# The quaternion memory read: POOL adds the components of two groups in pairs, PE sums two parts instead of four

## The reference, cut to what matters

```python
keys = (x @ Wk.T + bk).reshape(B, L, 32, 4)
keys = keys / jnp.maximum(norm(keys), 1e-12)
values = (x @ Wv.T + bv).reshape(B, L, 32, 4)
bound = quat_mul(values, keys)
memory = jnp.cumsum(bound, axis=1)
retrieved = quat_mul(memory, quat_conj(keys)).reshape(B, L, D)
retrieved = retrieved / jnp.sqrt(positions)[None, :, None]
normed = layernorm(retrieved) * ln_g + ln_b
return x + (normed @ Wo.T + bo)
```

## Time and profile before

| | us |
|---|---|
| time, median of 3 runs | 853.07 |
| lowest and highest of them | 850.7, 856.16 |
| the profiled execution: its time | 854.02 |
| the profiled execution: its span | 852.2 |
| PE busy in the span | 751.8 |
| DVE busy | 611.0 |
| POOL busy | 495.9 |
| ACT busy | 471.5 |

### The profile page before, as it was taken

How to read it: one execution, slowest core, us unless ns; L and a number is a source line. 1 busy time by engine, 2 the same in 40 slices (tenths; PEclk the granted TensorE clock), 3 DMA queues, 4 the chain that set the end, 5 groups by cost and what they waited for, 6 DMA issues and landing times.

```text
span 852.2 us, 14331 instructions
## 1 busy us (share of the span) xinstructions
PE 751.8 (88%) x3937; PEld 566.2 (66%) x3938; DVE 611.0 (72%) x1398; ACT 471.5 (55%) x951; POOL 495.9 (58%) x518
## 2 busy tenths in 40 slices
PE   4999999989674699917899987999999999999997
PEld 2444555545454699916888876787878787878785
DVE  3799999999843255534788775869686878787774
ACT  3465664556321477713666654666657565656453
POOL 3686776778545144423777764556565565655564
PEclk9999999999655799966999998999999999999999
DMA  8600000000001144520000006363829191918280
GB/s 234 226 2 1 0 1 2 12 4 10 13 26 35 44 123 117 144 62 25 13 14 1 1 2 142 60 145 70 166 48 190 28 197 31 191 44 174 49 165 13
DMA packets 40563, 60.19 MB, mean 71 GB/s; under 512 B 4033, under 2 KB 20033, under 8 KB 40241
## 3 DMA queue, kind: packets, MB, share of 16 engines
q1 hardware_dynamic: 38224, 54.73, 28.1%
q0 software_dynamic: 2272, 4.67, 1.6%
HBM read 51.11 MB, written 8.28 MB: 70 GB/s over the span
## 4 chain that ended last, share of the span: by engine, by line
PE 35%; DVE 9%; issue 3%; ACT 2%; DMA 1%; POOL 1%; POOLq 0%; DVEq 0%; SPq 0%; ACTq 0%
PE c_m L1498 3%; PE c_m L1500 3%; PE c_m L1499 3%; PE c_m L1463 2%; PE c_r L1479 2%; DVE c_bound L1797 2%; PE c_v L1498 1%; PE c_v L1499 1%; PE c_v L1500 1%; PE c_k L1498 1%; PE c_r L1549 1%; PE c_r L1552 1%; PE c_r L1550 1%; PE c_k L1500 1%; PE c_k L1499 1%
## 5 line engine op out<-in xcount | busy, mean ns | idle before, releaser
L2025 POOL TENSOR_TENSOR d_hid_lo<-c_bound,d_hid_hi 128x512 fp32r<-128x512 f32 x136 | 175.4, 1291 | 143.5 <-ACT d_hid_hi L1936 141.6
L1936 ACT ACTIVATE d_hid_hi<-c_bound 128x512 fp32r<-128x512 f32 x136 | 85.0, 625 | 38.8 <-DVE c_bound L1797 37.5
L867 POOL TENSOR_TENSOR a_rs<-a_r,a_state 128x512 f32<-128x512 f32 x64 | 75.1, 1183 | 37.5 <-DVE a_state L564 22.5
L564 DVE TENSOR_TENSOR_SCAN a_state<-a_decay,a_state,a_vb 128x512 f32<-128x512 f32 x64 | 80.9, 1266 | 0.1
L1071 POOL DMA_INDIRECT results<-b_y_row,b_result_row x39 | 37.2, 953 | 54.1 <-DVE b_y_row L1025 54.1
L1788 DVE TENSOR_TENSOR c_m<-c_bound,c_m 128x512 f32<-128x512 f32 x64 | 44.3, 692 | 24.0 <-PE c_m L1500 18.1
L1788 DVE TENSOR_TENSOR c_v<-c_bound,c_v 128x512 f32<-128x512 f32 x64 | 44.3, 692 | 21.9 <-PE c_v L1500 16.3
L1498 PE MATMUL c_m<-d_x_hi,d_hi 128*128 128x512 f32 x136 | 56.3, 414 | 3.7 <-DVE c_bound L1797 3.7
L1016 DVE TENSOR_TENSOR b_hidden<-b_h,b_b 128x512 f32<-128x512 f32 x39 | 27.0, 691 | 40.7 <-PE b_h L979 40.7
L1926 ACT ACTIVATE c_bound<-c_m 128x512 f32<-128x512 f32 x60 | 35.7, 595 | 33.6 <-PE c_m L1500 33.0
L1926 ACT ACTIVATE c_bound<-c_k 128x512 f32<-128x512 f32 x60 | 35.7, 595 | 33.3 <-PE c_k L1500 32.8
(11 more groups left out here) (310 smaller groups left out, 2159.4 us busy)
## 6 DMA issues: line engine op xcount, KB each, us to landing
d_w_wide<-pair_weights SPq DMA_DIRECT2D x64, 512.0 KB, 12.4
b_w<-in_w SPq DMA_DIRECT2D x2, 2048.0 KB, 11.7
d_w_wide<-in_moe SPq DMA_DIRECT2D x32, 102.0 KB
b_xin<-rows_in SPq DMA_DIRECT2D x39, 64.5 KB, 1.8
d_w_wide<-results SPq DMA_DIRECT2D x8, 256.0 KB, 2.8
out<-c_read SPq DMA_DIRECT2D x8, 256.0 KB, 2.2
a_weights<-in_mixing SPq DMA_DIRECT2D x1, 901.0 KB, 6.5
shape_consts<-in_consts SPq DMA_DIRECT2D x1, 744.0 KB, 4.7
```

The lines of the kernel that those rows point to most:

```text
L564: dve.tensor_tensor_scan(state[:, j, seq_cols(h, 1)], decay[:, h, :], vb[j % 3][:, :], first, ALU.mult, ALU.add).then_inc(scan_ready, 1)
L867: pool.tensor_tensor(rs[:, j, :], rr[:, h, :], state[:, j, seq_cols(h, 0)], ALU.mult).then_inc(rs_ready, 1)
L1936: act.activation(hid_hi[:, n % HALVES, :], hidden[:, r, :], ACT.Copy).then_inc(hi_ready, 1)
L2025: pool.tensor_tensor(hid_lo[:, n % HALVES, :], hidden[:, r, :], hid_hi[:, n % HALVES, :].bitcast(F32), ALU.subtract).then_inc(lo_ready, 1)
```

## The change

POOL gets one more operation in each body. After it has written the four products of groups 2 and 3, it adds the third and fourth to the first and second, in place, for both groups at once (128 x 2 x 256 numbers). A new semaphore `read_added` tells PE of it. PE then sums two parts instead of four with the identity for groups 2 and 3, and still four for groups 0 and 1. PE's wait for group 2 and for group 3 is now the same one, for the addition of both.

```diff
+        read_added = sem("read_added")
...
                         if s < 2:
                             pe.wait_ge(read_dve, 2 * i + s + 1)
                         else:
-                            pe.wait_ge(read_pool, 2 * i + s - 1)
-                        for m in range(QC):
+                            pe.wait_ge(read_added, i + 1)
+                        parts = QC if s < 2 else QC // 2
+                        for m in range(parts):
                             mm = pe.matmul(bank_r[:, s * P:(s + 1) * P], ident, read[:, s, m, :],
-                                           start=(m == 0), stop=(m == QC - 1))
+                                           start=(m == 0), stop=(m == parts - 1))
                         if s == SUB - 1:
                             mm.then_inc(read_out, 1)
...
                         for s in (2, 3):
                             pool.tensor_tensor(in_quats(read[:, s, :, :]), in_quats(key[:, h, s, :, :]),
                                                spread_component(memory_n[:, s - 2, :]), ALU.mult).then_inc(read_pool, 1)
+                        pool.wait_ge(read_pool, 2 * i + 2)
+                        pool.tensor_tensor(read[:, 2:, 0:2, :], read[:, 2:, 0:2, :], read[:, 2:, 2:, :], ALU.add).then_inc(read_added, 1)
                         need(pool, got_ready, i)
```

## The result

The changed kernel takes 856.56 us (median of 20 runs, 852.64 to 858.67) against 853.47 of the kernel before in the same comparison. The ratio is 1.0038, with a 95% interval of 1.0027 to 1.0048: 3 us slower, where 2.7 were forecast. Its profiled execution has a span of 855.5 us.

What follows compares the result with a forecast made beforehand. PE looked like the limit of the memory stage, with only 0.82 us of cover for POOL's addition. PE's waits for it, summed over the tiles, add 2.7 us to the 853.07 us median, giving 855.8; range 851.5 to 860.

Steps and rivals of the forecast that it cites:

- What bounds the kernel: Memory stage: PE is busiest, but POOL's products are ready only 0.82 us before PE wants them, the only cover.
- The addition: On POOL, 512 numbers a partition: 1.27 us, as `kept` takes, with bounds 1.09 and 1.78.
- the collision: DVE's second `d_lo` and POOL's addition wait for each other: 0.37 us more in each of tiles 2 to 6.
- What PE pays for the wait: From the addition's end to `got`: signal 0.06, eight passes after a wait 1.16, then 0.21, together 1.43 us.
- The sum, tile by tile: Later starts of `got`: tile 0 0.18, tile 1 0.31, tiles 2 to 5 1.76, tile 6 0.46; together 2.7 us.
- Tile 7: 0: Last tile of the stage: no gain or loss, covered by PE's 3.81 us idle until DVE gets weights from the DMA.
- one of the prediction's own signs of being wrong: In the changed kernel's profile, the granted clock falling below 1.00 in the memory stage would show the prediction wrong.
- the clock as a rival: PE's idle time, about 1 us a tile, lowers the clock; nearly 5 us per fall, two falls 865; chance 0.05.
- Balance: Rival: the addition escapes the collision, a tile takes 14.88 us, +0.8 in all, 852.7 to 854; chance 0.17.
- The full gain: Rival: PE never waits for the addition, 6.3 us less, 846.8; chance 0.07 together with halfway cases.

Runs made afterwards that it cites:

- the cut alone: Against the kernel before, PE sums only two of the four products of groups 2 and 3 and nobody adds the others; ratio 0.9932 (0.9909 to 0.9956).
- the addition alone: Against the kernel before, POOL adds in pairs into a spare tile nobody reads, PE still sums all four products; ratio 1.0008 (0.9988 to 1.0028).
- `d_lo` behind the addition: The changed kernel, with DVE's second piece of `d_lo` waiting for POOL's addition; ratio to the kernel before 1.0015 (0.9991 to 1.0039).
- group 2 alone: Against the kernel before, POOL adds in pairs only for group 2, PE sums four products of group 3; ratio 0.9979 (0.9954 to 1.0004).
- DVE adds: The change with its addition done by DVE at step 14 instead of POOL; ratio to the kernel before 1.0025 (0.9999 to 1.0051).
- the addition in two: The change with one addition for each of groups 2 and 3, each with its own signal; ratio to the kernel before 1.0030 (1.0007 to 1.0053).

## Why the prediction was right

- *What bounds the kernel.* Right. The cover between POOL's `read` and PE's use of it was read as 0.82 us; the addition needs 0.08 and 1.27, and the cut alone and the addition alone show each half of it: 0.9 us a tile to win, and 0.28 us in six tiles to lose, as long as PE does not wait.
- *The addition.* 1.27 us in tiles 0, 1 and 7, as `kept` had it. With the collision 1.63, forecast 1.27 + 0.37.
- *What PE pays for the wait.* 1.16 for eight passes, 0.06 of signal, 0.20 to `got`: 1.42, forecast 1.43. The signal's derivation has a slip (457.03 plus half of 1.28 leaves 0.09 to 457.76, not 0.05), but the 0.06 is what was measured.
- *The sum, tile by tile.* Tile 1 0.21 (0.31 forecast), tiles 2 to 5 0.56, 0.33, 0.55 and 0.32, as forecast to 0.01, tile 6 0.43 (0.46). Together 2.40 against 2.53. Tile 0, from POOL's `read` to `got`, 5.20 against 5.11: 0.09 (0.18).
- *Tile 7: 0.* This term was wrong, and one of the prediction's own signs of being wrong came true: the granted clock fell below 1.00 in the stage. The addition is covered there, but the fall came in front of the sixteen passes and cost 1.3 us on average on the chain. The prediction had named the clock as a rival, with PE's idle time as the cause and nearly 5 us as the price of one fall. One fall cost 0.8 to 1.6 us here, since it lasted 3.4 us and not 10, and the addition alone shows it without any new idle time of PE.
- *Balance.* The run with `d_lo` behind the addition gives +0.98 in tiles 1 to 6 in place of +2.40: without the collision more than half of the loss goes, and `real` becomes the limit. That case had +0.8 with tile 0.
- *The full gain* was there, but not by this way: 5.8 us with the cut alone, which leaves out half of a sum.

2.4 and 0.1 from the waits and 1.3 from the clock are 3.8 us, and the measured ratio means 3.2 (2.3 to 4.1), an interval that holds the forecast 2.7 too. The waits, 2.5 of the forecast 2.7, are shown tile by tile. That the whole time came as close is partly luck, since a term put at 0 measured 1.3. The rest of the span is no tool for the difference: from DVE's first use of the weights to the end the two first profiles differ by 0.4 us the other way.

## What to carry to other kernels

Work taken from the busiest engine is a gain only if that engine finds its operands when it gets there: read the cover, the time from the end of the producer to the consumer's start, and put the added operation with its wait against it. When it doesn't fit, give half of it (one group instead of two saved 0.45 us in each of tiles 2 to 5 without a wait), or give it to an engine that idles there, and look at what else that engine has in the one tile that differs from the others. A wait also costs the restart of what was pipelined, 0.27 us here for eight passes.

## What the runs showed of the hardware that was not expected

- A cast of 128 numbers a partition from float32 to bf16 on DVE waits for POOL as a two-input operation does. `d_strict` took 1.05 us where it was issued behind POOL's `read` (group 2 alone) and 0.37 in the kernel before; `d_ones` took 1.30 behind `bound` (DVE adds), 0.49 in the kernel before, where it met the shorter `real`, and 0.21 in the changed kernel, where it was issued before the addition.
- A DVE operation of 32 numbers a partition took 1.27 us behind POOL's `bound`, 0.45 in the kernel before beside `real`. It costs what is left of POOL's operation, not its own size.
- Not every two-input operation of POOL holds DVE up. In the kernel before, DVE's addition of 512 numbers with both inputs in SBUF (L1595, 430.48) took 0.68 us, issued behind a POOL power of 128x4 numbers that ran for 1.01 us (L2000, 430.35).
- The granted clock fell to 0.50 for 3.4 us in tile 7 in each of three profiles of the change and in those of the addition alone and the addition in two, never there in three profiles of the kernel before, while PE's work before the fall was the same in all of them. In DVE adds it fell in tile 2, after PE had been idle for 1.97 us.
